# Five orders of instructions written out anew, in a two-layer gated attention kernel on one core

## What is computed

```python
x = x + tanh(g_xattn[0]) * L0_xattn(layernorm(x), ctx, ctx, ...)   # 16 heads of 8, causal
x = x + tanh(g_ffn[0])   * L0_ffn(layernorm(x), ...)               # 6 experts, 100 tokens each, best one per row
x = x + tanh(g_xattn[1]) * L1_xattn(layernorm(x), ctx, ...)        # 8 heads of 64
x = x + tanh(g_ffn[1])   * L1_ffn(layernorm(x), ...)               # best 2 of 8 experts per sequence, 128-512-128, final norm
```

## Time and profile before

| | |
|---|---|
| runs | 248.61 us (median of 3; 246.94 to 249.54) |
| profiled execution | 246.28 us, of it 244.6 us from the first to the last instruction |
| PE, DVE, ACT, POOL busy | 84%, 62%, 56%, 39% of the span |
| mean granted clock of PE | 0.962 |
| DMA | 15.09 MB, mean 62 GB/s |
| first `S` on PE | 34.42 us |
| first `T` on PE | 49.32 us |
| last maximum of layer 0 ends | 72.9 us |
| first `pte` on PE | 85.87 us |
| last `av1` ends | 198.73 us |
| first `eo` begins | 212.31 us |

### The profile page before, as it was taken

The page is one execution under the profiler, slowest core; times in us unless marked ns, Lnnn a source line. Parts: engine busy times, 40 slices in busy tenths (PEclk is TensorE's granted clock), DMA queues, the critical chain, the costliest instruction groups (busy, mean ns, idle before and its releaser), DMA issues.

```text
span 244.6 us, 4582 instructions
## 1 busy us (share of the span) xinstructions
PE 205.9 (84%) x1626; PEld 146.4 (60%) x1626; DVE 151.0 (62%) x384; ACT 137.6 (56%) x343; POOL 94.4 (39%) x140
## 2 busy tenths in 40 slices
...
GB/s 122 325 54 236 187 259 255 121 4 3 3 5 4 3 0 3 0 0 3 0 1 4 0 0 0 3 0 3 0 160 39 186 9 0 222 168 21 24 23 21
DMA packets 13770, 15.09 MB, mean 62 GB/s; under 512 B 1316, under 2 KB 11300, under 8 KB 13748
## 3 DMA queue, kind: packets, MB, share of 16 engines
...
...
## 4 chain that ended last, share of the span: by engine, by line
PE 57%; DVE 21%; ACT 9%; POOL 5%; issue 3%; DMA 3%; SPq 1%; POOLq 0%; DVEq 0%; ACTq 0%
PE PS L1271 7%; DVE MX L735 6%; PE PS L1261 5%; ACT POOLED L620 4%; PE PS L1231 4%; PE PS L1202 4%; PE PS L1215 4%; PE PS L1179 4%; PE PS L1101 3%; PE PS L1039 3%; DMA CT<-in_ctxT 3%; DVE NM L832 2%; PE PS L1242 2%; PE PS L1188 2%; PE PS L1044 2%
## 5 line engine op out<-in xcount | busy, mean ns | idle before, releaser
L440 POOL TENSOR_TENSOR POOLED<-POOLED,RC 128x512 f32<-128x512 f32 x32 | 32.6, 1042 | 24.3 <-DVE RC L841 24.3
L735 DVE TENSOR_REDUCE MX<-PS 128x4 f32<-128x1024 f32 (+1 forms) x24 | 27.6, 1215 | 16.1 <-PE PS L1063 16.1
L620 ACT ACTIVATE POOLED<-PS,NM 128x256 f32<-128x256 f32 x64 | 29.5, 477 | 9.1 <-DVE NM L832 8.5
L429 POOL TENSOR_SCALAR_AFFINE_SELECT PT<-PT 128x512 f32<-128x512 f32 x16 | 10.2, 637 | 51.3 <-ACT PT L551 51.3
L551 ACT ACTIVATE PT<-PS 128x768 f32<-128x768 f32 x32 | 24.1, 809 | 10.5 <-PE PS L1082 10.5
L397 POOL TENSOR_SCALAR VE<-MV 128x2 f32<-128x2 f32 x20 | 5.1, 256 | 51.2 <-DVE MV L688 51.2
L1271 PE MATMUL PS<-POOLED 128*128 128x128 f32 x128 | 17.3, 293 | 5.0 <-ACT POOLED L662 5.0
L832 DVE TENSOR_REDUCE NM<-PS 128x4 f32<-128x1024 f32 x16 | 19.3, 1215 | 3.4 <-PE PS L1202 3.3
L1271 PEld LDWEIGHTS PS<-POOLED 128*128 128x128 f32 x128 | 16.9, 208 | 5.6 <-issue 5.3
L662 ACT ACTIVATE POOLED<-PS,BI 128x256 f32<-128x256 f32 x32 | 12.4, 479 | 13.8 <-PE PS L1261 13.8
L1202 PE MATMUL PS<-KT,VA 64*128 64x256 f32 x128 | 17.6, 399 | 2.1 <-ACT POOLED L620 2.0
...
## 6 DMA issues: line engine op xcount, KB each, us to landing
...
```

The source lines that it names most:

```text
L440: g_.tensor_tensor(pr, pr, RC1[:, n % 2, 2 * h:2 * h + 2].unsqueeze(2).to_broadcast([P, 2, S]), ALU.mult).then_inc(s_p1p, 1)
L620: last = a.activation(PR[n % 3][:, h, it, :], pair("sc", n)[:, h * 512 + it * S:h * 512 + (it + 1) * S], ACT.Exp, bias=NM1[:, n % 2, 2 * h ...
L735: v.tensor_reduce(MX0[:, b, it, :, hw * k:hw * (k + 1)], pair("S", n).rearrange("p (r h j) -> p r h j", r=2, h=hw), AXX, ALU.max, negate=T ...
```

## The change

The five tables are replaced by five others with the same entries in another order. Functions, instructions, tiles, semaphores and transfers are the same; only which piece follows which on an engine, and with it which piece of PSUM waits for which, is new. The order of the new tables was made from a list of dependences with measured durations, changes of the array's shape and the clock. Of the PE table the diff shows the first lines:

```diff
 PE_ORDER = table("""
-pk:0 xT:0:0 pk:1 pq:0 xT:0:1 pk:2 pk:3 pq:1 xT:0:2 kv:0:0 pq:2 xT:0:3 pq:3 tok:0 kv:0:1 kv:1:0 tok:1 kv:1:1 S:0
-S:1 S:2 S:3 S:4 S:5 kv:2:0 tok:2 S:6 mT:0 S:7 S:8 S:9 S:10 S:11 S:12 T:0:0 T:0:1 T:1:0 T:1:1 T:2:0 mT:1 T:2:1
+xT:0:0 xT:0:1 pk:0 pq:0 pk:1 pq:1 kv:0:0 xT:0:2 tok:0 xT:0:3 pk:2 pq:2 tok:1 pk:3 pq:3 kv:0:1 tok:2 S:0 S:1 S:2
+kv:1:0 S:3 S:4 S:5 kv:1:1 S:6 S:7 mT:0 S:8 kv:2:0 S:9 T:0:0 S:10 T:0:1 S:11 T:1:0 S:12 T:1:1 S:13 AV:0 T:2:0
...
 SP_ORDER = table("""
-so:0 so:1 si:0 si:1 so:2 late so:3 si:2 si:3 shift:0 shift:1 shift:2 shift:3 w12:0 w12:1 w12:2 w12:3 outd:0
+late so:0 so:1 si:0 so:2 si:1 si:2 shift:0 so:3 si:3 shift:1 shift:2 shift:3 w12:0 w12:1 w12:2 w12:3 outd:0
 outd:1 outd:2 outd:3
```

74 lines of the change are left out of this document (37 added, 37 removed).

## The result

The changed kernel takes 229.32 us (median of 4 runs, 228.25 to 230.72), the kernel before, run beside it, 247.98 us (median of 4, 246.94 to 249.54): a ratio of 0.925, 95% interval 0.917 to 0.933. The forecast was 237 us, 231 to 244.5. Times are medians of all runs, while the ratios and their intervals leave out disturbed runs, such as two of drain_two's four; the profiled one of to_tail_new was disturbed too.

A forecast was written before the change was run, and what follows sets the result against it. PE was taken as the bound nearly everywhere, so reordering returns only waits, slow stretches and ends. Terms summed to 11.2 us: 246.28 to 235.1, plus 2.3 to the median, 237.4, stated as 237 us, range 231 to 244.5.

The forecast's parts named there:

- Item 1: Start: pq:0 ahead of pk:1 brings so:0 to 14.6, and two transposes run in PE's waiting time; 0.9 us gained.
- Item 2: SP queue: late loads ahead of so:0 add 1 us; si:0 lands at 26.5, PE waits 1.9 us at S:0.
- Items 3 and 4: Front: braiding S and T cuts waits, 3.6 us gained; less time at the slow clock, 3.4 us gained.
- Item 5: Stretch from 71.2 to 86.6: of 1.85 us of PE waits, 1.5 us gained; bounds 0 and 1.85.
- Item 6: Long middle with 8.7 us of PE waits: no reason for more or fewer, 0 gained; bounds -4 and +4.
- Item 7: Tail, av1:15 to eo:0: 13.6 us becomes 12.6, 1.0 gained; eo:0 at a better clock, 0.8 more.
- From the execution to the median: End of the sum: 2.3 us added because the median lay that far above the profiled execution; 235.1 becomes 237.4.
- The clock did fall again: Rival: small waits bring slow-clock stretches back in front and tail, and a third comes; 241 us, chance 0.13.
- no middle gave back: Rival: in the middle, copies ahead of an e1 on ACT cost PE waits; 242 to 244 us, chance 0.10.
- DMA did not hold the front: Rival: si:0 lands near 30, so PE waits 5 us at S:0; 246 us, within 1%, chance 0.07.
- no e1 stood behind a copy: Rival, slower: in the middle an e1 stands behind an ACT copy once per sc; up to 264 us, chance 0.05.
- The rule weighed: PE, S and T: switching tiling mode drains the TensorE; 143 shape changes before, 140 now, 0.3 us, sum unchanged.

The follow-up runs named there:

- drain_two: The changed kernel with av1:4 and av1:5 moved ahead of sc:8 on PE; 230.9 and 231.7 us, too few for an interval.
- to_tail_new: The new order up to av1:15 and the order of the kernel before behind it; 234.32 us, ratio 0.944.
- late_back: The changed kernel with the late loads moved back behind so:2 on SP; 230.30 us, ratio 0.927.
- after_again: The changed kernel itself, unedited, run once more as a measure for later runs; 229.00 us, ratio 0.922.
- rest_new: The order of the kernel before up to the end of S:23, the new order behind it; 240.42 us, ratio 0.972.
- pe_mid: The kernel before with 16 pieces moved in PE's order alone, between val:1 and av1:15; 244.73 us, ratio 0.986.
- drain_full: The changed kernel with all that is left of batch 1's attention ahead of sc:8, other engines adjusted as needed; 237.98 us, ratio 0.960.

## Why the prediction was right or wrong

- **What bounds it: right.** Only waits, slow stretches and the ends could give, and they did: waits and ends 38.7 to 27.1 us, PE's busy time 205.9 to 201.3.
- **Item 1, start: right.** so:0 was issued at 14.51 (14.6 forecast), and PE was busy 1.3 us ahead of 8.9, where it had done nothing (0.9 forecast).
- **Item 2, SP: right in sum.** so:0 landed at 18.7 (19.7), si:0 at 26.9 (26.5), S:0 waited 2.1 us (1.9). The 1 us taken for the late loads was not there, as late_back shows. si:3 landed at 52.4 and S:18 began at 53.8 (48.5 and 51), inside the bounds.
- **Items 3 and 4, braid and clock: too large, and the sum right by luck.** Waits from 8.9 us to the end of S:23 fell from 6.6 to 3.9 us (3.0 forecast): 2.7 gained where 3.6 were forecast. The clock gave 2.0 (10.2 us of work at 0.50 before, 6.2 after), not 3.4. That S:23 came 7.8 us earlier, with 7.9 forecast, is due to item 1's extra 0.4, to AV:5, 0.9 us of work put off behind S:23, and to about 1 us less of busy time, whose cause stays open. The slow stretch was 6.8 us long, not 3.4, and began at 26.4, in the wait for S:0; T:0:0 came at 42.45 and not at 39.5, in good part for it. In after_again, with the same orders, there was none in the front, S:0 began at 26.8, T:0:0 at 39.92 and S:23 ended at 60.4 and not 63.4. 5.1 would have been the right size for item 4 in that execution; the item was uncertain by all it was worth.
- **Item 5: too large.** 0.7 us gained, not 1.5; waits 1.85 to 1.24.
- **Item 6, the middle: wrong, and most of the miss.** 7.4 us gained, not 0; waits 8.7 to 2.6. "No reason for more or for fewer: 0" rested on the work between one sc and its tp, 6.4 us now and 5.9 before, against a chain of 5.2. That weighed one path for all waits. In the old trace the waits of PE from 71 to 198.7 that end at that path's piece, tp, are these:

```profile
PE PS L1215 <- ACT POOLED L620: 1.6, 4, 0.6
```

Of the other 7 us, 2.0 stood at sc, 1.5 at xT:2:1, 1.4 at gate:2, and the rest at smaller places; the new order waits nowhere at tp for over 0.2 us. rest_new shows that the gain is the new order's own, whatever the front. pe_mid shows that small moves on PE alone take 3.3 us of these waits, and drain_full that the new order's 2.6 us hang on the overlap of two batches, which the tables show (in the old PE table sc:8 follows av1:7, in the new one av1:7 comes behind sc:11) and I did not look at. Which of its other placements gave how much stays open. The bound of +4, for which the prediction has no sum, was too narrow too.
- **Item 7, tail: wrong in sign, by 1.8 us.** 14.4 us, not 12.6. "hid:0 and hid:1 now run under the table load" assumed that the load goes as soon as the last exponential is done; it stands behind the wait for hid:0, which begins only behind r1:3 and ran at half clock: 1.45 us from r1c:3 to the load. The load of batch 1's experts was not late, as forecast. eo:0 took 2.02 us where it took 3.56; the stretch to the end of eo:7 gained 1.0, and 0.8 was taken.
- **From the execution to the median: wrong by 3.1 us.** I added 2.3 us because the profiled run of before was that much below the median of its runs. After the change the median was 0.8 below its profiled run (230.11); in after_again, the same kernel, it was 1.5 above (229.00 against 227.47). How a profiled run lies to the median of its kernel tells nothing of the next. The other 5.0 of the 8.1 us of miss (237.4 against 229.3) are the items: 7.4 of item 6, less what items 5 and 7 fell short.
- **The rivals.** The clock did fall again, but for less; no middle gave back; DMA did not hold the front; no e1 stood behind a copy to any effect. The rival that was missing is a middle that gains: the bounds of item 6 had it, the list didn't, so the range ended at 231.
- **The rule weighed** (the Trainium skill, TensorEngine Tiling (Array Packing), Tiling Modes) made no difference that a row shows: at full clock it was 0.54 to 0.75 us from the start of an S of six matmuls to that of the T behind it, beside 0.64 from one S to the next in the earlier trace rows.
